# Layer 1 attention with the two head parities on separate row halves of the array

## What is computed

```python
q = q * cos + _rotate_half(q) * sin
k = k * cos + _rotate_half(k) * sin
qg = q.reshape(b, HKV, G, t, DH)
scores = jnp.einsum('bhgtd,bhkd->bhgtk', qg, k) / math.sqrt(DH)
scores = jnp.where(causal[None, None, None], scores, jnp.finfo(jnp.float32).min)
attn = jax.nn.softmax(scores, axis=-1)
ctx = jnp.einsum('bhgtk,bhkd->bhgtd', attn, v)
```

## Time and profile before

| | us |
|---|---|
| median of 3 runs (1789.66 to 1794.48) | 1794.21 |
| span of the profiled execution | 1792.7 |
| PE busy | 1521.2 |
| DVE busy | 1148.1 |
| ACT busy | 607.1 |
| POOL busy | 340.2 |

### The profile page before, as it was taken

One profiled execution on the slowest core, in us unless ns is written; L12 is line 12 of the kernel. 1 busy time (PEld: TensorE's weight loads), 2 busy tenths in 40 slices (PEclk: granted clock), 3 DMA queues, 4 the chain that ended last, 5 costly groups with the idle time before them and its releaser, 6 DMA issues. The chain is left out here.

```text
span 1792.7 us, 24031 instructions
## 1 busy us (share of the span) xinstructions
PE 1521.2 (85%) x7034; PEld 1036.6 (58%) x7034; DVE 1148.1 (64%) x2429; ACT 607.1 (34%) x859; POOL 340.2 (19%) x382
## 2 busy tenths in 40 slices
PE   0399889898846881999999999699999999999969
PEld 0366657566535660777777776355555555555447
DVE  5576875768645455455555543688687786888527
ACT  4224223242223330111111111046456465666632
POOL 2243343334312230000000000012122121121211
PEclk9988979889767895999999999579899898999979
DMA  7200000100023432100000000402112111211032
GB/s 263 94 1 1 24 24 1 47 1 24 1 89 125 150 124 89 30 25 18 24 25 18 15 9 0 87 8 48 28 27 54 27 27 27 54 27 29 2 131 82
DMA packets 48596, 84.12 MB, mean 47 GB/s; under 512 B 8899, under 2 KB 16657, under 8 KB 48506
## 3 DMA queue, kind: packets, MB, share of 16 engines
q1 hardware_dynamic: 41874, 78.13, 15.0%
q10 hardware_dynamic: 6632, 4.97, 0.9%
HBM read 58.54 MB, written 24.26 MB: 46 GB/s over the span
## 5 line engine op out<-in xcount | busy, mean ns | idle before, releaser
L1515 ACT ACTIVATE f_prob<-f_bank 128x1024 f32<-128x1024 f32 (+3 forms) x384 | 304.4, 811 | 216.6 <-PE f_bank L1612 214.5
L1594 PE MATMUL f_bank<-f_kst,f_qst 96*128 96x512 f32 (+3 forms) x768 | 282.8, 412 | 24.9 <-DMA f_qst<-q_scr 12.5
L1535 DVE CUSTOM_DVE_ANT_0 f_bank<-f_bank,f_mask 128x128 f32<-128x128 f32 (+3 forms) x512 | 248.5, 503 | 79.5 <-PE f_bank L1594 64.0
L1594 PEld LDWEIGHTS f_bank<-f_kst,f_qst 96*128 96x128 f32 x768 | 153.0, 204 | 181.0 <-DVE f_mx L1535 62.3
L1612 PE MATMUL f_bank<-f_qst,f_kst 98*128 98x512 f32 (+3 forms) x768 | 217.0, 367 | 1.2 <-ACT f_prob L1515 1.2
L1483 POOL TENSOR_SCALAR_AFFINE_SELECT f_prob<-f_prob 128x256 f32<-128x256 f32 x256 | 104.0, 407 | 467.8 <-ACT f_prob L1515 467.2
L1538 DVE TENSOR_REDUCE f_mx_first<-f_bank 128x1 f32<-128x512 f32 x256 | 176.1, 688 | 17.4 <-issue 8.1
L1630 PE MATMUL f_bank<-f_prob,f_vst 128*32 128x512 f32 (+3 forms) x1536 | 169.3, 514 | 1.0 <-ACT f_prob L1515 0.8
L37 PE MATMUL d_bank<-xtl,d_wgh 128*128 (+1 forms) x352 | 143.1, 407 | 8.9 <-DMA d_zz<-z_gu_scr 8.9
L1612 PEld LDWEIGHTS f_bank<-f_qst,f_kst 98*128 98x128 f32 x768 | 135.2, 199 | 20.6 <-ACT f_prob L1515 9.3
L1187 ACT ACTIVATE d_hs<-d_bank 128x512 f32<-128x512 f32 (+1 forms) x44 | 26.3, 598 | 348.8 <-PE d_bank L39 348.8
(11 more groups left out here) (225 smaller groups left out, 2761.6 us busy)
## 6 DMA issues: line engine op xcount, KB each, us to landing
f_qst<-q_scr SPq DMA_DIRECT2D x32, 384.0 KB, 6.1
q_scr<-c_qh SPq DMA_DIRECT2D x32, 256.0 KB
wst<-L_ffn_w SPq DMA_DIRECT2D x6, 1024.0 KB, 6.5
f_kst<-k_scr SPq DMA_DIRECT2D x32, 192.0 KB, 5.2
d_qw<-L_ffn_qweight_gu SPq DMA_DIRECT2D x40, 128.0 KB, 2.6
xall<-L_attn_x SPq DMA_DIRECT2D x2, 2048.0 KB, 16.2
xb<-L_attn_x SPq DMA_DIRECT2D x4, 1024.0 KB, 5.6
x_d<-xb SPq DMA_DIRECT2D x4, 1024.0 KB, 4.3
```

The lines of the kernel that those rows point to most:

```text
L1515: act.activation(prob[:, c // 2 % 2, c % 2 * 2:c % 2 * 2 + 2, lo:], score_bank[c % 2][:, :, lo:], ACT.Exp, scale=D ** -0.5).then_inc(exp_d ...
L1535: dve.tensor_tensor_reduce(sc, sc, mask[:, CH - w:CH], 1.0, LEAST, ALU.add, ALU.max, mx[:, u, h % 2, h // 2, q:q + 1]).then_inc(spare_free, 1)
L1594: pe.matmul(spare[v][:, 0:w], qst[0:M_ROW, u, h // 2, q * P:q * P + P], kst[0:M_ROW, u, h % 2, at:at + w], start=True, stop=True).then_inc ...
```

## The change

The odd parity moves from rows 48 to 95 to rows 64 to 111, the second half of the array's 128 rows, and its maximum row stands behind it, on row 112; that of the even parity is row 48. There is only one key stack: the keys stand on rows 0 to 47 and once more on 64 to 111, with the -1 on rows 48 and 112. An item is a matmul over the 48 rows of its parity, a score matmul one over the 49 rows of its parity. The stack of the maxima is written with two DMAs as before. The order of the items is changed, so that even and odd parity alternate at equal width. The number of matmuls, their columns, and all waits are the same.

```diff
-M_ROW = 2 * PART
+HALF_ROWS = P // 2
...
-ITEMS = [(h, q, at, min(CH, (q + 1) * P - at)) for h in range(HG) for q in range(QB) for at in range(0, (q + 1) * P, CH)]
+ITEMS = [(2 * i + par, q, at, min(CH, (q + 1) * P - at)) for i in range(HG // 2) for q in range(QB)
+         for at in range(0, (q + 1) * P, CH) for par in range(2)]
+
+
+def stack_rows(par, extra=0):
+
+    return slice(par * HALF_ROWS, par * HALF_ROWS + PART + extra)
...
-        fixed = sb("fixed", [P, 2, 1])
-        qst = sb("qst", [P, STACKS, 2, T], F32R)
-        kst = sb("kst", [P, STACKS, 2, T], F32R)
+        fixed = sb("fixed", [P, 1])
+        qst = sb("qst", [P, STACKS, HG // 2, T], F32R)
+        kst = sb("kst", [P, STACKS, T], F32R)
...
-                    r = slice(par * PART, par * PART + PART)
-                    sp.dma_start(kst[r, u, par].bitcast(F32), k_scr[bass.ds(n, 1)].rearrange("n c d t -> (n c d) t")).then_inc(qk_in[u], 16)
+                    r = stack_rows(par)
+                    sp.dma_start(kst[r, u].bitcast(F32), k_scr[bass.ds(n, 1)].rearrange("n c d t -> (n c d) t")).then_inc(qk_in[u], 16)
...
-                    sp.dma_start(qst[M_ROW + par:M_ROW + par + 1, u].rearrange("o i (b q) -> o (i b) q", q=P).bitcast(F32),
+                    row = par * HALF_ROWS + PART
+                    sp.dma_start(qst[row:row + 1, u].rearrange("o i (b q) -> o (i b) q", q=P).bitcast(F32),
...
-                dve.tensor_copy(kst[:, u], fixed[:, :, :].broadcast_to([P, 2, T])).then_inc(cleared, 1)
+                dve.tensor_copy(kst[:, u], fixed[:, :].broadcast_to([P, T])).then_inc(cleared, 1)
...
-                pe.matmul(spare[v][:, 0:w], qst[0:M_ROW, u, h // 2, q * P:q * P + P],
-                          kst[0:M_ROW, u, h % 2, at:at + w], start=True, stop=True).then_inc(spare_ps, 1)
+                r = stack_rows(h % 2)
+                pe.matmul(spare[v][:, 0:w], qst[r, u, h // 2, q * P:q * P + P], kst[r, u, at:at + w],
+                          start=True, stop=True).then_inc(spare_ps, 1)
...
-                    mm = pe.matmul(score_bank[c % 2][:, hh, lo:], kst[0:M_ROW + 2, u, hh, k * P:k * P + P],
-                                   qst[0:M_ROW + 2, u, c % 2, h * CH + lo:(h + 1) * CH], start=True, stop=True)
+                    r = stack_rows(hh, 1)
+                    mm = pe.matmul(score_bank[c % 2][:, hh, lo:], kst[r, u, k * P:k * P + P],
+                                   qst[r, u, c % 2, h * CH + lo:(h + 1) * CH], start=True, stop=True)
...
-    fixed = np.zeros((P, 2, 1), f)
-    fixed[M_ROW, 0], fixed[M_ROW + 1, 1] = -1, -1
+    fixed = np.zeros((P, 1), f)
+    fixed[PART], fixed[HALF_ROWS + PART] = -1, -1
```

More of the change, by code:

```diff
@@ L1455, in step @@
                     load(third)
-            sp.dma_start(fixed[:, :, :], fixed_d).then_inc(fixed_in, 16)
+            sp.dma_start(fixed[:, :], fixed_d).then_inc(fixed_in, 16)
             for u in range(STACKS):
```

## The result

The changed kernel takes 1889.35 us (median of 4, 1885.65 to 1895.62), the kernel before 1791.93 beside it: ratio 1.054, interval 1.0514 to 1.0568. The forecast was 1743 us, faster than before; the change costs 97 us instead. The profiled execution has a span of 1893.9 us.

A forecast was written before the change was run, and what follows sets the result against it. PE was taken as the bound (busy 31.85 of 32.20 us a group), with DVE right behind. Savings in copies, prologue, groups, boundaries and last stretches summed to 50.9 us: 1794.2 - 50.9 = 1743 us, range 1729 to 1784.

The forecast's parts named there:

- Score pairs overlap: Attention stage: both score matmuls of a chunk run side by side, 0.26 us instead of 0.48, saving 4.4 us of PE per group.
- Rival B: Attention stage: the halves don't overlap, PE stays the bound and shape changes cost 8 us; 1802 us, chance 0.10.
- ten plain groups x 2.7: Attention groups without a loop boundary: each saves 2.7 us, from 32.2 to 29.5, 27.0 us together.
- Rival C: After a loop boundary the clock stays at 1.2 GHz, 38 us a group; 1876 us, chance 0.05.
- The group at 1.2 GHz: Attention group at the low clock after the change: PE needs 36 to 40 us, against some 54 before.
- The group at full clock: Attention group at 2.4 GHz: 29.5 us instead of 32.2, taking 2.7 of 3.7 us that DVE waits for PE.
- rival A: Attention groups: PE's single stream ties DVE and ACT, 31.0 us a group; 1766 us, chance 0.18; sign: DVE waits above 2 us.
- 2 us of item overlap: Item matmuls of alternate parities partly overlap, saving 2 us of PE per group, within bounds of 0 to 4.5.
- Order of the items at nothing: DVE's same 48 items a group in another order: no new wait, uneven spread of one to three per chunk 0 on average.
- Change of shape at the turns: 128x128 turns between 64-row work: 4 more steps a group, each 0 to 0.15 us, together 0.5 us of PE.
- The last stretches: End of the attention stage: 1.6 us saved from 1663.96 to 1684 and 2.4 us from 1684 to 1717.
- Boundaries: Three groups with a loop boundary: each saves 2.0 us there besides 2.7, 14.1 us together; first excess 10.4 down to about 8.

The follow-up runs named there:

- e12_rows64_old_order_unrolled: The changed kernel with halves filled by zero rows to 63 and 64 rows, the earlier item order and the loop written out: 1749.09 us, ratio 0.9742.
- e6_rows64: The changed kernel with each half filled up with zero rows, items over 63 rows and scores over 64: 1796.62 us.
- e2_one_half: The changed kernel with both parities on the first row half, so nothing can overlap by rows: 2134.35 us.
- e14_after_unrolled: The changed kernel with the hardware loop written out, so without loop boundaries: 1878.26 us.
- e10_old_order: The changed kernel (48 and 49 rows) with the items in the order of the kernel before: 1990.08 us, ratio 1.111.
- e1_order: The kernel before with only the new order of the items (parities alternate): 1824.88 us.
- e9_rows64_old_order: The changed kernel with halves filled to 63 and 64 rows and the items in the order of the kernel before: 1791.54 us, ratio 0.9989.

## Why the prediction was wrong, point by point

- *What bounds the kernel:* right for the kernel before. In the changed one PE is the bound again, through its clock (busy 40.63 of 42.24 us in a group).
- *Score pairs overlap:* right. 0.43 us for two at 1.2 GHz instead of 0.85. At 2.4 GHz a pair of 512 costs 0.35 (1566.56 to 1566.91 in e12_rows64_old_order_unrolled) instead of 0.48, not the 0.26 forecast. Rival B is out.
- *The step that failed: "ten plain groups x 2.7", and every other term for whole groups.* They took over the granted clock of 1.00 from the trace of before. The part-by-part list had columns, shapes, waits and copies for each matmul and no entry for the rows. But the rows went from 96 and 98 to 48 and 49, and with them the clock of a group went from 1.00 down to between 0.56 and 0.77; plain groups take 38 to 43 us instead of the 29.5 forecast. Filling the halves up with zero rows brings 1889 back to 1797 us (e6_rows64); the few rows without overlap give 2134 (e2_one_half).
- *Rival C* had the effect and a price near the truth, 1876 for 1889.35, but not the cause or the place, and the price is near by luck: it had 38 us a group with the clock at 0.50 throughout from the first boundary on, and the groups take 38 to 45 us with the clock going up and down. e14_after_unrolled has no boundary and still takes 1878. I had argued against it that TensorE "would again be the bound" at 1.2 GHz and so rise; e2_one_half shows TensorE busy without a gap for over 780 us at 0.50.
- *The group at 1.2 GHz,* put at 36 to 40 us: 42.56 in the changed kernel with the clock at 0.56, and 47.63 at 0.50 in the old order (e10_old_order), where item matmuls don't overlap each other.
- *The group at full clock,* put at 29.5 us: the change with filled halves takes 31.15 (e6_rows64, PE busy 27.73, DVE 26.95), where rival A had put 31.0; so even at full clock a group would have gained 1.05 us and not 2.7. DVE's waits for PE stay at 2.8 us in it, above the 2 us named as the sign of A. With the old order it is 30.46 (e12_rows64_old_order_unrolled), PE busy 29.37 of it and DVE 26.57. The assumed 2 us of item overlap was wrong for the old order, and the part of rival A that says PE's stream stays tight was right.
- *Order of the items at nothing:* wrong, 1.67 us a group at full clock in the kernel before (e1_order), of which 1.33 are idle time of PE (1.68 of 33.87 us instead of 0.35 of 32.20). With filled halves it is 0.3 to 0.5 us (31.15 in e6_rows64, 30.62 and 30.82 at the same places in e9_rows64_old_order). How it comes about is open: two items beside each chunk instead of one to three didn't help.
- *Change of shape at the turns, 0 to 0.15 us:* from the turn to the next score pair 0.55 us (1566.01 to 1566.56), 0.41 in the earlier trace rows: 0.14 more, at the upper end; two other turns have 0.58 (e12_rows64_old_order_unrolled, 1586.71) and 0.59 (e6_rows64, 1328.17), a little over it. It was not what decided. The Trainium skill, "TensorEngine Tiling (Array Packing)", Key Properties, says that a change of the tiling mode drains TensorE; the added time agrees with that.
- *Copies:* 1.90 us instead of 3.50, right. *Prologue:* the 1.0 us isn't there; from the first to the second values' copy it is 50.82 us, 50.83 before.
- *The last stretches,* put at 1.6 and 2.4 us saved: the clock is at 0.50 from 1718.5 to 1790.5, and from the last copy to the end of the program it is 137.75 us instead of 128.74. Rival C had some 8 us more there.
- *Boundaries:* predicted to cost less after the change. They cost more where the clock was held otherwise (up to 49.8 us a group in e9_rows64_old_order), since there the clock takes longer to come back.

The Trainium skill, "TensorE: Matmul & The Clock Gate", Why this matters for your kernels, advises to keep TensorE continuously busy to get to the high clock. In e2_one_half, busy 56.43 of 56.43 us in a group, that didn't suffice; the measurement decides.

## What to carry to other kernels

Before matmuls are cut to fewer rows, or moved to one half of the array, take the granted clock as a term of the sum with a price of its own, and try the same matmuls filled up with zero rows: here the zeros were worth 93 us. Give overlapped halves their full 64 rows and read PEclk group by group before any other row; a busy TensorE is no sign that it runs at 2.4 GHz. And a loop boundary that stalls all engines can be paid twice: once as the stall, once as the stretch at 1.2 GHz behind it. Written out, the kernel before gained 31 us (1795.02 to 1763.56), the one with filled halves and the old order 42 us (1791.54 to 1749.09).

## What the runs showed of the hardware that I had not expected

- TensorE busy without a gap at 1.2 GHz for fourteen groups: 48- and 49-row matmuls one after the other take 56.4 us a group at 0.50, and 63- and 64-row ones too; 96- and 98-row ones take 32.2 us at 1.00.
- Rows of zeros on overlapping halves move the clock: mean of the run 0.807 to 0.817 without, 0.894 with them, same columns and same values.
- More work can be less time: 384 more pairs of score matmuls made the changed kernel 44 us faster (one execution).
- The clock fell within work, with PE busy 3.74 of the 4 us before.
